# Cross-attention with a routed expert layer: the value products of four head pairs in one place, an expert block and an expert sum moved up

## What is computed

```python
x = x + attention(ctx, _layernorm(x), mask)   # queries from x, keys/values from ctx and x: 333 keys
# q = ln @ W_q; k, v from [xn @ W_kv, ln @ W_kv]; 4 heads of 64; q and k RMS-normalized
# attn = softmax(masked sim); out = (attn @ v) @ W_out + b_out
y = _layernorm(x)
# router: sigmoid scores, best group of 4 of 8 experts, best 2 in it, weights cw
# routed = sum_e cw[e] * relu(y @ up_e)^2 @ down_e;  shared = relu(y @ up_s)^2 @ down_s
x = x + routed + shared
```

## Time and profile before

| | before |
|---|---|
| runs | 1273.66, 1275.27, 1275.74 us (median 1275.27) |
| profiled execution | 1275.34 us, span 1273.5 us |
| PE busy | 1188.7 us (93%), 10176 products |
| DVE busy | 1057.6 us (83%), 3593 instructions |
| ACT busy | 747.8 us (59%) |
| POOL busy | 540.2 us (42%) |
| granted TensorE clock, mean | 0.989 |

### The profile page before, as it was taken

One profiled execution on the slowest core, in us unless ns is written; L12 is line 12 of the kernel. 1 busy time (PEld: TensorE's weight loads), 2 busy tenths in 40 slices (PEclk: granted clock), 3 DMA queues, 4 the chain that ended last, 5 costly groups with the idle time before them and its releaser, 6 DMA issues.

```text
span 1273.5 us, 29626 instructions
## 1 busy us (share of the span) xinstructions
PE 1188.7 (93%) x10176; PEld 1102.2 (87%) x10176; DVE 1057.6 (83%) x3593; ACT 747.8 (59%) x1733; POOL 540.2 (42%) x477
## 2 busy tenths in 40 slices
PE   3699999999999999999999999999999999999996
PEld 2589988898988889988889988889988889988886
DVE  3688888898888888888888888888888888888875
ACT  3566555666655666655666655666655666655652
POOL 3244444444444444444444444344444344444332
PEclk9699999999999999999999999999999999999999
DMA  5000000000000000000000000000000000000000
GB/s 147 12 13 21 21 21 9 13 21 21 21 20 10 12 21 21 21 21 11 12 21 20 21 21 18 5 21 21 21 21 21 2 21 21 21 21 21 2 10 17
DMA packets 28228, 25.86 MB, mean 20 GB/s; under 512 B 6640, under 2 KB 27536, under 8 KB 28080
## 3 DMA queue, kind: packets, MB, share of 16 engines
q1 hardware_dynamic: 27744, 23.83, 5.9%
q0 software_dynamic: 336, 0.14, 0.2%
HBM read 15.57 MB, written 8.39 MB: 19 GB/s over the span
## 4 chain that ended last, share of the span: by engine, by line
PE 46%; issue 25%; DVE 11%; POOL 9%; ACT 8%; DMA 1%; ACTq 0%; POOLq 0%; DVEq 0%
POOL hid_lo L1177 6%; PE up_ps L261 4%; PE attn_ps L261 4%; PE attn_ps L371 4%; PE up_ps L263 4%; PE down_ps L261 4%; PE up_ps L262 4%; PE attn_ps L262 4%; PE attn_ps L263 3%; ACT probs L617 3%; PE down_ps L263 3%; PE down_ps L262 3%; ACT relu_sb L657 2%; POOL rstd L1134 2%; PE attn_ps L310 2%
## 5 line engine op out<-in xcount | busy, mean ns | idle before, releaser
L1177 POOL TENSOR_TENSOR hid_lo<-relu,hid_hi 128x512 fp32r<-128x512 f32 x192 | 247.6, 1289 | 321.3 <-DVE hid_hi L984 321.3
L261 PE MATMUL down_ps<-down_hi,hid_hi 128*128 128x256 f32 x768 | 230.2, 300 | 44.2 <-DVE acc L999 38.7
L261 PE MATMUL up_ps<-x_hi,up_hi 128*128 128x256 f32 x768 | 225.3, 293 | 1.4 <-ACT x_hi L646 1.2
L999 DVE SCALAR_TENSOR_TENSOR acc<-down_ps,route_w,acc 128x256 f32<-128x256 f32 x512 | 217.3, 474 | 3.7 <-PE down_ps L263 2.8
L263 PE MATMUL down_ps<-down_hi,hid_lo 128*128 128x256 f32 x768 | 217.4, 283 | 0.0
L262 PE MATMUL down_ps<-down_lo,hid_hi 128*128 128x256 f32 x768 | 216.7, 282 | 0.0
L262 PE MATMUL up_ps<-x_lo,up_hi 128*128 128x256 f32 x768 | 214.2, 279 | 0.0
L263 PE MATMUL up_ps<-x_hi,up_lo 128*128 128x256 f32 x768 | 214.1, 279 | 0.0
L617 ACT ACTIVATE probs<-masked,neg_max,q_scale 128x333 f32<-128x333 f32 x256 | 168.9, 661 | 63.9 <-DVE neg_max L839 63.9
L261 PEld LDWEIGHTS down_ps<-down_hi,hid_hi 128*128 128x128 f32 x768 | 146.0, 190 | 56.4 <-issue 56.4
L657 ACT ACTIVATE relu_sb<-up_ps 128x512 f32<-128x512 f32 x192 | 113.1, 589 | 110.9 <-PE up_ps L263 110.8
(11 more groups left out here) (147 smaller groups left out, 2867.1 us busy)
## 6 DMA issues: line engine op xcount, KB each, us to landing
x_in<-in_x SPq DMA_DIRECT2D x32, 256.0 KB, 2.7
out<-acc SPq DMA_DIRECT2D x32, 256.0 KB, 2.2
c_in<-in_ctx SPq DMA_DIRECT2D x32, 77.0 KB
up_stage<-in_up_t SPq DMA_DIRECT2D x1, 1536.0 KB, 12.7
down_stage<-in_down_t SPq DMA_DIRECT2D x1, 1536.0 KB, 15.8
mask_in<-in_mask SPq DMA_DIRECT2D x32, 9.6 KB, 2.8
w_stage<-in_w_kv SPq DMA_DIRECT2D x1, 512.0 KB, 5.7
w_stage<-in_w_q SPq DMA_DIRECT2D x1, 256.0 KB, 5.1
```

Source lines behind the costliest of these rows:

```text
L261: nc.tensor.matmul(out_ap, s_hi, m_hi, start=first, stop=False)
L999: nc.vector.scalar_tensor_tensor(acc[:, t, :], down_ps[:, (e + 1) % 2, t * D:(t + 1) * D], route_w[:, t, e:e + 1], acc[:, t, :], ALU.mult, ...
L1177: nc.gpsimd.tensor_tensor(hid_lo[:, p % HID_RING, :], relu2[:, p % 2, :], hid_hi[:, p % HID_RING, :], ALU.subtract).then_inc(hid_lo_done, 1)
```

## The change

On PE, the first two calls of probs_times_v leave their place behind down(1) and go behind spread_inverse, ahead of the other two; up(5) goes ahead of down(2). On DVE, add(1) goes ahead of normalize1. Nothing is added or removed otherwise; the waits inside the functions are the same.

```diff
@@ PE, step @@
                 ffn("up", 4)
                 ffn("down", 1)
-                probs_times_v(b, 0)
-                probs_times_v(b, 1)
                 transpose_probs(b, 4)
                 transpose_probs(b, 5)
                 transpose_probs(b, 6)
+                ffn("up", 5)
                 ffn("down", 2)
-                ffn("up", 5)
                 ffn("down", 3)
                 if following:
                     transpose_ln(b + 1, experts)
...
                 ffn("down", 4)
                 ffn("down", 5)
                 spread_inverse(b, following)
+                probs_times_v(b, 0)
+                probs_times_v(b, 1)
                 probs_times_v(b, 2)
                 probs_times_v(b, 3)
@@ DVE, step @@
                 widen_inverse(b, 0, first)
                 high(4)
+                add(1)
                 if following:
                     normalize1(b + 1, False)
-                add(1)
                 invert_sums(b, 1)
                 widen_inverse(b, 1, first)
                 add(2)
```

## The result

| | before | after |
|---|---|---|
| median of 8 runs | 1275.51 us | 1279.59 us (1277.79 to 1280.89) |
| profiled execution's span | 1273.5 us | 1276.8 us |
| ratio | 1 | 1.0032, 95% interval 1.0021 to 1.0043 |

The change makes the kernel slower by 0.32%, 4.1 us. I had forecast 1277.4 with a range of 1271.5 to 1285.5, called "the same" the likeliest verdict (0.43), and slower nearly as likely (0.40). The mechanism was the one of the forecast; its price was too small.

A forecast was written before the change was run, and what follows sets the result against it. Bound: a per-step ring through PE and DVE, with the normalization's end hanging on POOL. Thirty steps +2.4 us, first step 0, last -0.3: sum +2.1, so 1277.4 us, range 1271.5 to 1285.5.

The forecast's parts named there:

- The ring: Each step runs from the normalization's end along PE to the next up(0), then along DVE to the next normalization's end.
- kv1: PE's first key/value products in a step, forecast at 627.58 instead of 627.50.
- Values behind the reciprocals: PE: 1.65 us leave the stretch ahead of down(2); the later value visit grows from 1.46 to 2.77 us.
- up(5) ahead of down(2): PE: the order costs nothing; up(5) takes 1.5 us and covers the wait for POOL's low(3).
- add(1), and E unmoved: DVE: add(1) fills a 0.42 us wait; the normalization starts at 619.69 instead of 619.40 but still ends at 621.42.
- E: The end of DVE's normalization in a step, 621.42, said to hang on POOL's low(4).
- What is late next: PE behind the normalization: waits of 0.9 us before the transposes and 0.25 before down(4), then blocks and values to 627.58.
- third wait: PE ahead of down(4), waiting for DVE's add(2): 0.25 us, down(4) starting at 622.77.
- Per step: Each of thirty steps +0.08 us, +2.4 us in all.
- The clock: Slower rival: PE's waits halve its clock in some steps; 3 of 30 give 1282 us; chance 0.30 together with E moving.
- The tail: Faster rival: DVE's product of attention and reciprocals starts earlier, -0.28 us a step, 1267 us; chance 0.12.
- That E moves by 0.29: Slower rival: the normalization ends 0.29 us later, +0.37 a step, 1286 us; chance 0.30 together with the clock.

The follow-up runs named there:

- e1: Kernel before with only DVE's add(1) moved ahead of the normalization: 1240.18 us (ratio 0.9727).
- e7: e5 with all value products in one visit ahead of down(4), transpose 7 behind down(2), high(3) ahead of the normalization's statistics, ACT's copy earlier: 1251.76 us.
- e4: Changed kernel with up(5) put back behind down(2): 1280.24 us (ratio 1.004).
- e5: e3 with DVE's high(4) moved behind add(1) and the normalization, so POOL's low(4) doesn't run beside the normalization: 1261.99 us (ratio 0.9895).
- e3: Changed kernel with DVE's second pair of reciprocal operations moved behind add(3): 1266.80 us (ratio 0.9939).
- e6: Kernel before with add(1) ahead of the normalization and the second reciprocals behind add(3), no moves on PE: 1229.57 us (ratio 0.964).
- e9: Repetition of e6, same code, against the kernel before: 1227.94 us (ratio 0.9642).
- e2: Kernel before with only value products 0 and 1 moved behind the reciprocals: 1314.61 us (ratio 1.0306).

## Why the prediction came out as it did

**What bounds the kernel: right.** The ring held in every kernel, in that wherever kv1 moved, the step moved with it: the stretch from kv1 to the next up(0) is 10.54 us before and 10.54 after (38.02 - 27.48 and 38.18 - 27.64), 10.51 in e1 and 10.49 in e7.

**Values behind the reciprocals: right.** 2.77 us for 48 products, as computed, and the block behind the nine transposes at 618.03, 17.04 behind up(0), against 17.08 expected (617.06 - 599.98).

**up(5) ahead of down(2): right,** shown by e4.

**add(1), and E unmoved: right.** The normalization's pair starts 0.3 us later and ends as before. That low(4) is what holds it was an argument; e5 shows it, with 0.74 us for the pair when low(4) isn't there. The rule of the Trainium skill, SBUF — State Buffer, section "Who interferes with whom", agrees in its main point, that the second to come is blocked rather than slowed: starting 0.3 us later cost nothing (E within 0.02 us). The same page says in section "SBUF: two separate sides" that a DVE operation with two inputs in SBUF also waits for a POOL operation that reads SBUF. For add(1) I had gone by the row of before (0.88 beside 0.86), and it held; of its two large inputs one, down_ps, is in PSUM. Both inputs of the pick in e7 are in SBUF; there I had not thought of the rule, and 0.17 became 1.17 us.

**What is late next: right in place, short by 0.06 us.** The term that was mis-sized is "add(3) ends at 623.45 and frees down(5) at about the same moment; down(5) 0.71". "About the same moment" was taken as no wait, so I used the 0.71 us of an uninterrupted block, though with the 0.15 us from add's end to PE that I used elsewhere down(5) would have come out at 623.60, 0.04 late. After, down(5) starts at 624.54, 0.15 behind add(3)'s end, and the spread at 625.32, 0.78 later. The first product is not late (0.12 behind the last of down(4), as in any block), but the second comes 0.19 us behind the first instead of 0.12. How much depends on how late the release is: where add(3) ends 0.15 us ahead of down(5) the second product is 0.19 behind (after, e1, e4), at 0.19 it is 0.15 behind (e3), at 0.27 and more 0.12 (before, e6; medians). Why PE loses it there is not shown, and a wait is not the only thing that goes with it: down(4) of the kernel before, behind transposes and with all inputs ready for 0.6 us, has 0.20 too.

From E to kv1 the forecast had 6.16 us (621.42 to 627.58), the changed kernel has 6.22 (622.40 to 628.62). The long waits too differ from the text: 0.6 in front of the transposes instead of 0.9, since they start 0.06 behind E and not 0.15, and since the printed idle time is less than the distance between two starts (0.62 is printed where the products start 0.90 apart, 621.56 and 622.46); this changed nothing, as down(4) waits for add(2) anyway. This third wait is there, though no row prints it and the wait for `acc` above (10.9 us, 30 times) is down(3)'s alone: down(4) starts 0.41 us behind the last transpose in the median, where it was 0.03 before, and 0.15 behind add(2)'s end, in the place that was forecast (1.35 behind E). e3 takes it away and kv1 comes sooner.

**Per step and in sum.** +0.08 was forecast, the mean of the 30 steps is +0.155. About 0.06 of the missing 0.075 us is this late second product; the rest, some 0.015, lies in E, and I have not traced it. Over 30 steps it is 1.8 us: with it the forecast would have been 1279.2, past the 1277.8 that I had counted as the same. The stretch up to up(0) of step 1 is 1.33 shorter where I had taken 0 in a range of -1.5 to +1.3. That this comes from the change is not shown: e1, which up to that product does what the kernel before does, has it at 66.27, 1.10 us sooner than before.

```profile
66.27 0.36 PE L261 MATMUL up_ps<-x_hi,up_hi 128*128 128x256 f32 x1 [0.20 <-DVE x_lo L901]
```

The end stayed as it was, not 0.3 shorter.

**The rivals.** The clock did not fall in the steps of the changed kernel. The granted clock (third figure from the end) is 1.00 in a window over the three waits, and in one from step 0 to the last step:

```profile
619.00:623.00 4.00, 3.02 (x23) 2.57 (x23) 3.97 (x11) 1.96 (x5) 2.61 (x3) 1.00 0.00 0
52.10:1236.00 1183.90, 1149.03 (x9864) 1063.54 (x9866) 1004.97 (x3456) 710.39 (x1674) 515.82 (x433) 1.00 0.06 17
```

The tail did not shorten either: the attention product came 0.19 us earlier behind up(0) (27.81 against 28.00) and kv1 to up(0) stayed 10.54, so DVE's product of attention and reciprocals had slack. That E moves by 0.29 is refuted above.

## What to carry to other kernels

When one wait comes back in every step, find the event that ends it and split the work by that event: what stands behind it is paid, what stands ahead of it within the wait is free. So a move from ahead to behind undoes the gain of an earlier release, even if it saves work on the busiest engine, and two edits that are bundled should each be tried alone: here one was worth -35 us and the other +39. Price a release that comes just in time as well: here it cost PE 0.07 us in one block of each step.

## What the runs showed that I had not expected

A POOL subtraction of 128x512 that begins 0.15 us ahead of a DVE operation on 16 elements with both inputs in SBUF holds that up for 1.0 us (0.174 to 1.173 us, e7).

The 0.33 us that one step took longer is not random: the long steps are loop steps 3, 22 and 26 in the trace of every kernel here but e7, where step 26 has its usual length. After the change the same two spreads as in the earlier trace rows, of steps 21 and 22, are 38.55 us apart instead of 38.35:

```profile
854.23 0.60 PE L387 MATMUL up_ps<-ident,inv_wide 128*128 128x128 f32 x4
...
892.78 0.60 PE L387 MATMUL up_ps<-ident,inv_wide 128*128 128x128 f32 x4
```

The prediction had put it on DVE's side, and the trace of before agrees: E is 0.33 later in these steps, and in step 26 DVE stands still for 0.48 us in front of one small operation, where it is 0.14 in step 25.

```profile
1034.90 0.20 DVE L750 TENSOR_SCALAR mask_row<-mask_in 128x77 f32<-128x77 uint8 x1 [0.48 <-DVE stats L744]
```

What holds it there was not tried and stays open.

The clock can fall in step 1, and not in every execution of a kernel. This is the same window in the traces of e6 and of e9, which are the same kernel (the first row shows 0.50, the lower level, 1.2 GHz):

```profile
66.30:73.10 6.80, 6.80 (x33) 6.58 (x33) 1.07 (x4) 1.76 (x4) 3.82 (x3) 0.50 0.18 52
66.30:73.10 6.80, 6.61 (x58) 6.30 (x59) 3.55 (x17) 2.77 (x6) 4.17 (x3) 1.00 0.21 52
```

Ahead of it PE stood still in both for 1.00 us in front of the second normalization's transposes and for 0.20 in front of up(0). Step 1 lasts 39.6 us in e6 and 36.5 in e9. The traces of e2 and e4 have such a step too, 3.0 and 3.1 us over their median step. So 3 us in the total of a single trace say nothing about an edit here; that is why the steps are compared by their medians. What decides it is not shown.
